# Head attention of a two-layer transformer block: the two row scores of a half key tile moved in front of its first column score

## The reference

```python
q = einsum('oc,bct->bot', Wq, target) + bq      # b = 8, 256 channels, t = 512
k = einsum('oc,bcs->bos', Wk, source) + bk
v = einsum('oc,bcs->bos', Wv, source) + bv
# 16 heads of 16 channels
dot  = einsum('bhdt,bhds->bhts', q, k) / 4
dot  = mask * dot - (1 - mask) * 1e6
amap = softmax(dot, axis=-1) * mask
out  = einsum('bhts,bhds->bhdt', amap, v)
```

## Time and profile before

| what | us |
|---|---|
| median of three runs | 1444.24 (1442.85 to 1448.8) |
| the profiled execution: its own time | 1444.01 |
| its span, first to last instruction | 1442.2 |
| head attention, TensorE's loop over the sequences | about 200.7 to 676.8 |
| one whole sequence in the middle | 58.7 to 58.8 |

### The profile page before, as it was taken

How to read it: one execution, slowest core, us unless ns; L and a number is a source line. 1 busy time by engine, 2 the same in 40 slices (tenths; PEclk the granted TensorE clock), 3 DMA queues, 4 the chain that set the end, 5 groups by cost and what they waited for, 6 DMA issues and landing times.

```text
span 1442.2 us, 23319 instructions
## 1 busy us (share of the span) xinstructions
PE 1304.6 (90%) x9113; PEld 752.4 (52%) x9142; DVE 1018.3 (71%) x1523; ACT 649.0 (45%) x941; POOL 297.1 (21%) x473
## 2 busy tenths in 40 slices
PE   4787868888988988886999989999999999999998
PEld 2343412222222222223768766777777767777776
DVE  8989779889898897884778846644467544575353
ACT  5675537778777877883453111132111221112210
POOL 1008255545465554320000000000000000000000
PEclk9999979999999999997999999999999999999999
DMA  6300222323334323233744301000010000200000
GB/s 196 113 18 16 75 74 86 114 82 107 104 96 144 100 81 93 70 103 105 254 129 148 100 30 59 16 15 1 30 60 2 30 1 15 68 8 30 1 1 30
DMA packets 78039, 101.23 MB, mean 70 GB/s; under 512 B 14680, under 2 KB 51648, under 8 KB 77928
## 3 DMA queue, kind: packets, MB, share of 16 engines
q1 hardware_dynamic: 75879, 99.43, 21.8%
q0 software_dynamic: 2048, 0.27, 0.1%
HBM read 78.07 MB, written 21.34 MB: 69 GB/s over the span
## 4 chain that ended last, share of the span: by engine, by line
PE 41%; DVE 8%; DMA 1%; issue 1%; ACT 1%; POOL 1%; POOLq 0%; DVEq 0%; SPq 0%; ACTq 0%
PE double L1800 13%; PE double L1814 11%; PE double L1826 6%; PE double L1879 3%; PE double L1847 3%; PE double L1836 3%; PE double L1866 1%; PE double L1784 1%; DVE stats L1987 1%; DVE hid L2034 1%; DMA x_early<-scr_x 1%; DVE gate L2032 1%; DMA out_x<-x_early 1%; DVE x_early L2003 1%; POOL rstd L1973 1%
## 5 line engine op out<-in xcount | busy, mean ns | idle before, releaser
L1029 ACT ACTIVATE prob<-level,head_scale 128x512 f32<-128x512 f32 x512 | 318.9, 682 | 91.0 <-PE level L946 90.9
L1390 DVE TENSOR_REDUCE nmx<-level 128x2 f32<-128x1024 f32 x256 | 304.8, 1221 | 56.1 <-PE level L936 55.8
L1912 ACT ACTIVATE th<-double 128x512 f32<-128x512 f32 x96 | 53.9, 562 | 386.3 <-PE double L1800 213.2
L946 PE MATMUL level<-stacks 59*128 59x512 f16 x512 | 174.1, 387 | 24.7 <-ACT prob L1029 24.4
L936 PE MATMUL level<-stacks 57*128 57x512 f16 x512 | 149.9, 392 | 12.2 <-DVE nmx L1390 11.5
L1800 PE MATMUL double<-x_parts,f0w 128*128 128x256 f16 x1408 | 157.6, 275 | 1.6 <-PEq L521 1.6
L374 PE MATMUL level<-prob,x_parts 128*128 128x448 bf16 (+1 forms) x527 | 123.7, 387 | 38.4 <-DVE prob L421 16.9
L1973 POOL TENSOR_TENSOR rstd<-meanvar,halfpow 128x2 f32<-128x2 f32 x22 | 15.2, 691 | 688.5 <-DVE meanvar L1993 688.5
L1800 PE MATMUL double<-x_parts,f1w 128*128 128x256 f16 x1408 | 155.2, 273 | 0.4 <-DVE hid L2034 0.4
L1800 PEld LDWEIGHTS double<-x_parts,f0w 128*128 128x128 bf16 x1408 | 138.9, 99 | 20.6 <-issue 2.2
L1800 PEld LDWEIGHTS double<-x_parts,f1w 128*128 128x128 bf16 x1408 | 137.5, 98 | 18.5 <-DVE hid L2034 0.6
(11 more groups left out here) (254 smaller groups left out, 1873.4 us busy)
## 6 DMA issues: line engine op xcount, KB each, us to landing
stacks<-scr_q SPq DMA_DIRECT2D x64, 96.0 KB
stacks<-scr_k SPq DMA_DIRECT2D x64, 96.0 KB
hid<-in_f1w1t SPq DMA_DIRECT2D x8, 704.0 KB, 6.4
hid<-in_f1w2t SPq DMA_DIRECT2D x8, 704.0 KB, 4.2
inputs<-in_x SPq DMA_DIRECT2D x8, 512.0 KB, 7.2
inputs<-in_ctx SPq DMA_DIRECT2D x8, 512.0 KB, 7.0
scr_q<-splits SPq DMA_DIRECT2D x16, 256.0 KB, 2.4
scr_k<-splits SPq DMA_DIRECT2D x16, 256.0 KB, 2.2
```

The costliest lines, as they stand in the source:

```text
L946: nc.tensor.matmul(pB[n % 2], Ks[rows, g, j // 2, P * c:P * (c + 1)], Qs[rows, g, j // 2, :], start=True, stop=True).then_inc(s["b_pe"], 1)
L1029: nc.scalar.activation(prob[:, c, j, :], pB[(64 * b + 16 * g + 4 * c + j) % 2], ACT.Exp, scale=hscale[:, 10:11]).then_inc(s["exp_done"], 1)
L1390: nc.vector.tensor_reduce(nmx[:, g % 2, :, half, tt], pA[(32 * b + 8 * g + u // 2) % 2], AX.X, ALU.max, negate=True).then_inc(s["max_done" ...
L1912: y = nc.scalar.activation(th[:, 0:m, :], src[:, 0:m, 0:S], ACT.Tanh, scale=0.5 / XS)
```

## The change

In each half key tile the pair of row scores is issued before the first of the two column scores, and the pair's two members change places: h = 0 first, then h = 1. TensorE's order in a tile becomes pair, C0, C1, job, pair, C2, C3, V, job. What is computed, the number of instructions, the buffers, and the waits of each call stay as they are; the other engines' streams are the same but for the order in which a pair's two halves are written.

```diff
         def row_unit(u):
-            j = u % 4 ^ 1
+            j = u % 4
             return j % 2, j // 2, u // 4
...
                         for half in range(2):
-                            column_scores(b, g, c, 2 * half)
                             if not (last and next_one):
                                 row_scores(nb, ng, u0 + 2 * half)
                                 row_scores(nb, ng, u0 + 2 * half + 1)
+                            column_scores(b, g, c, 2 * half)
                             column_scores(b, g, c, 2 * half + 1)
```

## The result

The changed kernel takes 1458.57 us (median of 6 runs, 1456.04 to 1462.88) against 1445.93 for the kernel before (6 runs): ratio 1.0090, 95% interval 1.0068 to 1.0111, so 12.6 us slower. Timed again later, it gave 1457.68 against 1445.88, ratio 1.0078 (1.0057 to 1.0099), 11.8 us. The forecast was +11.6 us, 1455.8 us in all, with a range of 1452.5 to 1459; it was made on a median of 1444.24 for the kernel before, which three more runs moved to 1445.93. In the experiments the ratios and intervals leave out three executions in a far slower state (1707.15 and 2476.62 us among 23 of the kernel before, 1691.66 among six of experiment 7), the medians do not: without them these are 1445.00 and 1436.66.

What follows compares the result with a forecast made beforehand. No engine is full; a chain through PE and ACT (C0, exponentials, C2, C3, V) bounds the tile. Sequences 0 to 5 cost 7.8 us, sequence 6 1.5, sequence 0's extra 0.4, the last 1.9: 11.6, or 1455.8 us, range 1452.5 to 1459.

Steps and rivals of the forecast that it cites:

- The sum: Whole kernel: 1.30 us for a sequence, 11.6 us in total, giving 1455.8 us.
- C0 one slot late: Start of a plain tile: the pair takes the first slot, C0 starts 0.22 us late, tile 3.28 and not 3.06.
- Pair in front of C2 costs nothing: Second half tile: the pair runs while PE waits for the exponential; cost 0, also where it waits in (1,3) and (0,3).
- Which tiles pay: Per sequence: (2,0), (3,0), (3,3), (2,1), (3,1) +0.22 us each, (3,2) +0.20; (2,2) with (2,3) gives 0.20 back; others 0.
- the sum is 11.6 and not 8.8: VectorE's L1419 ends with GpSimd's product through the shared port: sum 11.6 us; were the length VectorE's own, 8.8.
- First and last sequence: Sequence 0 pays 0.4 us more in (0,2) and (0,3); the last pays 1.9 over nine tiles with row scores.
- Cost 0, if that holds: Dropping the `^ 1`: halves still alternate 0, 1, 0, 1, so four scores still take two slots; cost 0.
- VectorE as the bound: Rival: VectorE bounds the kernel and earlier row scores feed it, faster by 24 us (1420) or 20 us; chance 0.07.
- Most given back: Rival: waits in group 2 and tile (3,0) swallow most of the loss, +5 us, 1449; chance 0.15.
- Packing lost: Rival: scores do not pack in array halves in the new order, C0 at 0.43, twice the loss, 1467; chance 0.06.
- The clock: Rival: TensorE's granted clock falls, V doubles, about 1.2 us a tile, ten tiles add 12 us, 1468; chance 0.03.

Runs made afterwards that it cites:

- experiment 7: Kernel before, with V of tiles c = 0 and 3 issued as 256 queries behind C1 and 256 behind C3: 1437.02 us, ratio 0.9955.
- experiment 1: Against the kernel before, new order only in the first half of each tile (pair in front of C0): 1459.11 us, ratio 1.0101.
- 2: Against the kernel before, new order only in the second half of each tile (pair in front of C2): 1445.86 us, ratio 1.0002.
- 5: Changed kernel with the pair in front of C0 issued twice: 1475.02 us, ratio 1.0208 to the kernel before.
- 3: Kernel before, order C0, pair, C1 kept, only the pair's two members swapped: 1445.92 us, ratio 1.0006.
- 4: Pair moved in front of C0 and C2 as in the change, members kept in the old order: 1458.95 us, ratio 1.0104 to the kernel before.
- 8: Kernel with V cut in two, tiles c = 2 cut as well, first half behind the transposes t: 1441.82 us, ratio 0.9970 to the kernel before.
- experiment 6: Against the kernel before, the pair behind both column scores in each half tile (C0, C1, pair; C2, C3, pair): 1455.02 us, ratio 1.0076.

## Why the prediction was right

*The sum.* From the projection of v ahead of the first sequence to the last o the changed kernel's profile takes 499.06 us, before 484.60: +14.5. The long end of the stage is 3.1 of it, the rest 11.4. In the second profile of the changed kernel it is 495.58, +11.0, without a long end. The forecast was 11.6. The 1.0 us by which the first median lies above it can come from the long end, since five of those six runs have clocks of 0.972 to 0.974; only one of them has a profile, and the runs of the kernel before are mixed as well. That the medians lie within 1 us of the forecast is therefore in part luck; that 11.0 to 11.4 us of it arrived in the tiles is not.

*C0 one slot late.* Put at 0.22, measured 0.23 at 436.29; tile 3.28, as written. Shown to be the cause by leaving it alone (experiment 1: all of the loss), leaving it out (2: none) and doubling it (5).

*Pair in front of C2 costs nothing.* Right (2), cover and all: the stop grew in (1,3), V did not move.

*Which tiles pay.* Group 0 and 1: 16.57 us between the q's, unchanged. In tile (0,1) the exponential still stands behind the evacuation of k, as in the earlier trace rows; C0 came 0.23 later and nobody noticed:

```profile
444.32 0.78 ACT L1012 ACTIVATE splits<-pM,bks,head_scale 128x512 f32<-128x512 f32 x1 [1.00 <-PE pM L878]
444.44 0.38 PE L946 MATMUL level<-stacks 59*128 59x512 f16 x2
...
445.00 1.26 ACT L1029 ACTIVATE prob<-level,head_scale 128x512 f32<-128x512 f32 x2
```

Group 2 to v0: +0.48 for 0.44; v1 to the next q: +0.88 for 0.86. The starts of V, counted from the first q of a sequence, say it tile by tile: in groups 0 and 1 they move by 0 but for (0,2) and (1,2), which are 0.2 later and give it back in the next tile; in group 2 they move by 0.22, 0.44, 0.65 and then 0.48, in group 3 by 0.66, 0.87, 1.09 and 1.30. Tile (0,2) shows from the other side what the earlier trace rows showed, VectorE's instruction ending with GpSimd's: L1419 starts earlier against GpSimd than before and is longer by as much.

```profile
389.68 1.61 DVE L1419 SCALAR_TENSOR_TENSOR rs<-rs,mcol 128x16 f32<-128x16 f32 x1
389.99 1.27 POOL L1102 TENSOR_TENSOR splits<-splits,mrow 128x512 f32<-128x512 f32 x1
```

It ends at 391.29, GpSimd's product at 391.26. Before, it took 1.43 us and ended as closely. VectorE's head start of 0.2 us is used up inside the instruction, so the sum is 11.6 and not 8.8. The Trainium skill, page GPSIMD Engine Reference, section Key points, says that GpSimd shares its SBUF interfaces with VectorE and contends with VectorE's instructions that have two SBUF inputs. The trace agrees: L1419 has two, and it ends 0.03 us behind GpSimd's product in both kernels, with 0.12 or 0.31 us of head start. The wait of v0 on `O` was 0.31 us at the weight load, before 0.48: `O` came late together with the rest, as forecast.

*First and last sequence.* The first q's interval was put at +0.4 and measured +0.06 here and +0.43 in experiment 1 (+0.21 in the second profile of the changed kernel); it partly runs at the lower clock level in every kernel, and its size is not told apart from that. Sequence 6 pays 0.65 from q(1,0) to its first v (25.20 against 24.55) where the forecast's tiles give 0.64, and 1.51 from its second v to the first o of the last sequence (25.31 against 23.80) where they give 1.50. The six tiles from there to the last row scores pay 1.30 (23.06 to the job of L906, against 21.76), as forecast.

*One condition was wrong.* "Cost 0, if that holds": the swap costs 0, but not because the halves alternate; without alternation it costs 0 too (3, 4).

*The rivals.* VectorE as the bound: excluded by 2, where it is fed earlier and nothing changes. Most given back: no, 11 of 11.6 us arrived. Packing lost: no, 0.23 and not 0.43. The clock: in the changed kernel it stayed at 1.00 in the sequences behind the first; the lower level lasted longer at the end of the stage in some runs, and that is not bound to the order. The rival was real all the same: in experiments 7 and 8 a V in the middle of the head attention took 1.85 to 1.88 us.

## What to carry to other kernels

In a ring of two engines, find the stretch that nothing covers (here from C3 over V to the first column score and its exponential) and the one where TensorE waits anyway (here C1 to C2). An instruction is free in the second while there is room and costs its full slot in the first, at whichever end of it it stands and unless another wait covers it (tiles c = 1 in experiment 6), however idle the engines look on average; and work moved out of the first into the second wins time, as cutting V in two did (6.5 us). Before a gap is filled, count what already stands in it (tiles c = 2), and afterwards look at the granted clock of every sequence, not of one in the middle.

## What was not expected of the hardware

Two scores on the same half of the array, issued next to each other with two of the other half behind, had the same recorded starts (0, 0.01, 0.23 us) and the same time for the whole as alternating ones. And the granted clock at the end of the stage, after TensorE has stood idle for 5 to 7 us, comes back at different moments in runs of one kernel: the last V pair took 1.92 or 3.40 us, worth 3 us in all, a quarter of what this change did. With V cut in two the clock also fell once or twice inside the sequences, after a stop of 0.96 us behind which it stayed up one sequence later.
